# Routing turns on TensorE: float32 products with the identity in place of transposes

## The reference

```python
h = layernorm(x)
theta = relu(mean(gcn(h, edges)))            # one vector of 64
coefs = ...sigmoid(theta @ W2 + b2)...       # [256, 4]: two scales, two shifts per channel
x = x + max(h * scale0 + shift0, h * scale1 + shift1)      # per channel
h = layernorm(x)
top, idx = top_k(h @ gate_w + gate_b, 2)     # 16 experts
y = h + sum_k softmax(top)_k * (relu(h @ w1[idx_k] + b1) @ w2[idx_k] + b2)
x = x + layernorm(y) * gamma + beta
```

## Time and profile before

| what | us |
|---|---|
| three timed runs | 886.05, 889.9, 895.62 (median 889.9) |
| span of the profiled execution, first to last instruction | 882.4 |
| TensorE busy, matmul records / weight loads | 741.0 / 643.2 |
| VectorE / ScalarE / GpSimd busy | 676.2 / 475.4 / 282.7 |
| mean granted clock of TensorE over the span, as a share of full speed (no time) | 0.913 |

### The profile page before, as it was taken

One profiled execution on the slowest core, in us unless ns is written; L12 is line 12 of the kernel. 1 busy time (PEld: TensorE's weight loads), 2 busy tenths in 40 slices (PEclk: granted clock), 3 DMA queues, 4 the chain that ended last, 5 costly groups with the idle time before them and its releaser, 6 DMA issues.

```text
span 882.4 us, 21305 instructions
## 1 busy us (share of the span) xinstructions
PE 741.0 (84%) x6322; PEld 643.2 (73%) x6322; DVE 676.2 (77%) x1837; ACT 475.4 (54%) x1199; POOL 282.7 (32%) x313
## 2 busy tenths in 40 slices
PE   3555788888885776897899999999999999998893
PEld 3555355555555765876889999999998999997682
DVE  6999699999963688776757777777776777775597
ACT  5995677777635675653334444444444444443253
POOL 8400000000000457777734544544422222223010
PEclk9999699999997676568999999999999999999796
DMA  9850444445616944459999999899999999893999
GB/s 270 223 162 1 130 148 152 165 142 175 172 64 237 227 133 145 128 152 292 254 278 280 267 264 263 266 264 261 269 254 335 323 260 273 262 262 116 353 319 200
DMA packets 156240, 192.82 MB, mean 219 GB/s; under 512 B 78235, under 2 KB 125262, under 8 KB 153036
## 3 DMA queue, kind: packets, MB, share of 16 engines
q1 hardware_dynamic: 127048, 109.40, 44.7%
q10 hardware_dynamic: 15448, 51.04, 17.4%
q0 software_dynamic: 13632, 31.03, 11.2%
HBM read 151.05 MB, written 40.34 MB: 217 GB/s over the span
## 4 chain that ended last, share of the span: by engine, by line
PE 60%; DVE 23%; issue 8%; DMA 3%; ACT 3%; SPq 2%; DVEq 0%; ACTq 0%; POOL 0%; POOLq 0%
PE PS L1296 21%; PE PS L1308 19%; DVE W L1357 8%; PE PS L1334 4%; DVE W L1388 3%; DVE W L1423 3%; PE PS L1090 3%; PE PS L1186 2%; PE PS L1201 2%; DMA R<-xs 2%; PE PS L1214 2%; PE PS L1110 2%; SPq L719 2%; PE PS L1054 1%; DVE st L1464 1%
## 5 line engine op out<-in xcount | busy, mean ns | idle before, releaser
L1296 PEld LDWEIGHTS PS<-R,W 128*128 128x128 f32 x1808 | 223.1, 195 | 17.2 <-DVE R L1640 11.9
L1296 PE MATMUL PS<-R,W 128*128 128x128 f32 x1808 | 225.1, 278 | 9.7 <-DVE R L1640 9.7
L992 ACT ACTIVATE R<-PS,b1T 128x128 f32<-128x128 f32 x350 | 102.9, 367 | 233.9 <-PE PS L1296 233.8
L1308 PE MATMUL PS<-W,R 128*128 x904 | 213.9, 380 | 0.0
L610 POOL DMA_INDIRECT ys<-W,R x113 | 109.7, 971 | 230.9 <-DVE W L1692 228.5
L1308 PEld LDWEIGHTS PS<-W,R 128*128 128x128 f32 x904 | 163.6, 191 | 17.4
L1357 DVE TENSOR_TENSOR W<-R,W 128x3136 bf16<-128x3136 bf16 (+1 forms) x104 | 157.2, 1571 | 0.7 <-PE PS L1070 0.7
L890 ACT ACTIVATE W<-PS 128x1024 f16<-128x1024 f32 x104 | 106.2, 1023 | 38.0 <-PE PS L1090 32.0
L603 POOL DMA_INDIRECT xs<-W,slot_i x98 | 101.8, 1039 | 75.0 <-DVE slot_i L1522 46.3
L1090 PE MATMUL PS<-W,table 114*128 114x512 f16 x208 | 66.3, 403 | 26.3 <-DVE W L1388 25.9
L595 POOL MEMSET R<- 128x261 f32 x1 | 0.3, 317 | 226.4 <-PEq L1132 226.4
(11 more groups left out here) (264 smaller groups left out, 1028.9 us busy)
## 6 DMA issues: line engine op xcount, KB each, us to landing
W<-in_L_ffn_w ACTq DMA_DIRECT2D x96, 512.0 KB, 5.0
W<-key_rows SPq DMA_DIRECT2D x26, 784.0 KB
W<-in_L_ffn_w SPq DMA_DIRECT2D x33, 512.0 KB, 8.5
R<-xs SPq DMA_DIRECT2D x113, 130.5 KB
W<-ys SPq DMA_DIRECT2D x4, 2048.0 KB, 13.0
R<-xs SPq DMA_DIRECT2D x224, 32.0 KB
XH<-in_x SPq DMA_DIRECT2D x6, 896.0 KB, 11.7
W<-xs SPq DMA_DIRECT2D x116, 32.0 KB
```

Of the source, the lines that this page charges most:

```text
L992: last = act.activation(HT3[:, u, j, :], up_out(u, j), ACT.Relu, bias=b1T[:, ds(e, 1), j])
L1296: last = nc.tensor.matmul(up_out(u, j), W1S[b][:, k, j * P:(j + 1) * P], XT3[:, u, k, :], start=(k == 0), stop=(k == 1))
L1308: last = nc.tensor.matmul(PS[:, 6 * u, 0:C], HT3[:, u, j, :], wt2(e * W2COLS, j), start=(j == 0), stop=(j == 3))
```

## The change: what it does

The three calls of `nc.tensor.transpose` in `turn1`, `back` and `turn2` become `nc.tensor.matmul` with the same three operands (the block as the stationary side, the 128x128 float32 identity as the moving side). A transpose is that product with a flag set; now the flag is left out, and each turn is an ordinary float32 product. Operands, PSUM places, waits, signals and the order on each engine stay as they were. Other transposes of the program (in the graph stage and in `turn_tables`) stay as they were too.

```diff
-                            last = nc.tensor.transpose(TA[q % 2][:, j, k, :], XH[:, DG[g][0] + j0 + j, k * P:(k + 1) * P], ident[:, :])
+                            last = nc.tensor.matmul(TA[q % 2][:, j, k, :], XH[:, DG[g][0] + j0 + j, k * P:(k + 1) * P], ident[:, :],
+                                                    start=True, stop=True)
...
-                            last = nc.tensor.transpose(TB[:, j, k * P:(k + 1) * P], bra[q % 2][:, k, j, :], ident[:, :])
+                            last = nc.tensor.matmul(TB[:, j, k * P:(k + 1) * P], bra[q % 2][:, k, j, :], ident[:, :],
+                                                    start=True, stop=True)
...
-                            last = nc.tensor.transpose(PS[:, 6, j * C + k * P:j * C + (k + 1) * P],
-                                                       xn[:, g % XNBUFS, 2 * b + j, k * P:(k + 1) * P], ident[:, :])
+                            last = nc.tensor.matmul(PS[:, 6, j * C + k * P:j * C + (k + 1) * P],
+                                                    xn[:, g % XNBUFS, 2 * b + j, k * P:(k + 1) * P], ident[:, :],
+                                                    start=True, stop=True)
```

## The result

| | before, on the same chip | after |
|---|---|---|
| median of four timed runs, us | 887.97 (884.33 to 895.62) | 906.02 (901.56 to 914.89) |
| span of the profiled execution, us | 882.4 | 905.3 |
| its own timed value, us | 884.33 | 907.03 |
| mean granted clock over the span | 0.913 | 0.940 |

The account below looks back on a forecast made before the run. The routing stage was taken as bound by TensorE at a mostly half clock. Turns +5.6, gates -5.5 and cold starts +2.6 gave +2.7 us on 889.9: 892.5 us, range 882 to 909.

Parts of the forecast that it names:

- half clock behind 360 us: Sign of being wrong: the profile after still shows half clock there, where near 1.00 was expected from 340 to 390 us.
- the last `back`: End of the routing stage's turns: expected within 4 us of where it was, at 383.93 us before.
- The bound: Routing stage, 262 to 455 us: bound by TensorE more than any other engine, at a clock mostly half; expert steps follow.
- Turns and gates: Routing chain: 230 turns as full-clock products plus hand-over tails, +5.6 us; 109 gate records cheaper at full clock, -5.5 us.
- Cold starts: Products beginning at half clock after long waits at three places, 0.9 us each: +2.6 us, bounds 0 and 5.2.
- The rival that the clock falls at every `back`: Routing stage: each of 13 `back`s on the chain starts and stays cold, 18.6 us more, 908.5 us; chance 0.13.
- The rival that the clock's pattern stays: From 262 to 390 us the mean clock stays 0.645, products cost 40.8 us more, gates gain nothing: 931 us; chance 0.10.
- GpSimd's sends: Back to back from 330.09 to 434.85 us: ending some 4 us later, ahead of the fourteenth step's need, costed at nothing.

Follow-up runs that it names:

- experiment 1: Products of zeros put in TensorE's waits of the routing stage, in the changed kernel: 896.76 us, ratio 1.007 to the kernel before.
- experiment 5: Changed kernel, waits filled, 18 zero products ahead of the last group: 893.76 us, ratio 1.0036; transposes likewise, plus 14 before the second expert step: 878.75 us, 0.9847.
- experiment 2: The same products of zeros in the same waits, in the kernel before with its transposes: 886.54 us, ratio 0.9894.
- `turn2` alone: Only `turn2`'s 98 turns made products, in the kernel before: 901.75 us, ratio 1.0099.

## Why the prediction was right in its range and wrong in its sum, step by step

The time lies in the range (882 to 909), but 13.5 us above the forecast and outside the forecast's own bounds (885 to 900). The range holds it only because it was widened for a rival that had 0.13, with other places and prices than the runs showed; that is luck in good part. Slower by over 1%, which came, had 0.23. Of the signs of being wrong, half clock behind 360 us came (0.50 from 362.54 us to 373.76), and the last `back` begins 12.6 us later, not within 4.

**The bound** was read rightly: the stage is limited by TensorE, and what the last `back` lost, the expert steps lost with it.

**Turns and gates** (+5.6 and -5.5 us). The prices held: 16 records in 1.95 us to their end, gates at 0.96 us for eight. With the clock held by fillers the change costs 0.36% of the median, 3.2 us, where these two terms sum to +0.1; its stage is 2.0 us longer than before. So experiments 1 and 5 bear the two terms out together, to some 2 or 3 us, with the fillers' own cost included; neither was measured alone.

**Cold starts** (+2.6 us, bounds 0 and 5.2) is the step that failed, by size. It measured 11.1 us in the stage (after against experiment 1) and about 3 at the last group (experiment 1 against 5), 14 in all. Put in place of 2.6, the forecast's sum of 2.7 becomes 14.1 us; by the ratio the change costs 16 us, by the medians 18, and the two stretches ahead of the second expert step differ by 16.1. Three things in it were wrong:

- The places. I took three, `back` at 275 and behind `fill_soon` and the first `prefix`, and all three fell. Three more did, at 329, 346 and 387, behind waits of 2.28, 1.87 and 3.25 us. I had argued from the expert steps, which kept 1.00 over waits of 1 to 2 us up to 445 us. The next wait behind that window, of 2.20 us, already speaks against it (before, from the timeline):

```profile
445.93 3.55 PE L1296 MATMUL PS<-R,W 128*128 128x128 f32 x16 [2.20 <-DVE R L1640]
```
- The length. I took half of one `back`'s 1.73 us. The fall at 362 lasted from `back` through the gates, `turn1` and the next `back`, 11 us.
- The work already there for this. Of `spin` I had only named that it exists. At full clock the same eight products end 1.7 us sooner, the wait behind them opens, and the clock falls where before it had just come up.

**What would have been seen from the rows ahead.** The rival that the clock falls at every `back` (908.5 us) came nearest to the time, with 0.13; it had too many places (of the 15 `back`s, 6 fell behind a wait), and made each too short. Its 13 waits of 1 to 5 us were misread, too: the timeline of before has 11, of 0.45 to 4.78 us, and 7 of them reach 1 us. The rival that the clock's pattern stays (931 us) is refuted by the windows of after. The Trainium skill (Perfetto Trace Analysis, section Transposes) asks for transposes rather than products for every logical transpose. At equal fillers the runs agree: 1.018 in time for the products (experiments 1 and 2). What I had weighed was a turn at the clock of before against a product at full clock; the runs show that the turn gains from fillers as well, though its clock is held less well, and then it is the cheaper one.

**GpSimd's sends** at nothing: the last one is issued at 449.24 us, against 434.85, and the fourteenth `up`, the first whose rows wait for the sends, takes 1.95 us at 471.64 with no wait ahead in TensorE's timeline. That held.

**What stays open**: some 2 to 4 us of the cost, which lie in the price of the turns, in the expert steps or in the scatter of the medians; why waits of 1.87 and 2.28 us lose the clock and one of 2.63 us doesn't; and why the clock of `turn2` alone falls below that of before.

## What to carry to other kernels

When an edit is to pay through the clock, first price what the old form gains when the clock is raised in another way: here, with the same fillers, the transposes were ahead by some 1.8%, although their clock still fell at times. Waits of 1.9 to 6 us between short stretches of mixed work on TensorE cost the clock in six places here, and the price of a fall is all the work until the clock climbs, not one instruction; filling such waits with products of zeros gave 1.5% on the kernel as it was. Whatever already keeps the clock up (here `spin`) is sized for the clock that it finds, and must be sized anew when that changes.

## What the runs showed of the hardware that was not expected

- Turns lose the clock in work that products hold it through. In experiment 2 it falls at 298 us while TensorE works without a gap. In experiment 1, with the same fillers ahead, the same gates stand between products and keep their full-clock length, as does the `back` behind them:

```profile
302.32 0.96 PE L1223 MATMUL PS<-gw_sb,W 128*128 128x16 f32 x8
303.17 0.71 PE L1208 MATMUL PS<-ident,W 128*128 128x128 f32 x4
303.72 0.96 PE L1223 MATMUL PS<-gw_sb,W 128*128 128x16 f32 x8
304.53 1.58 PE L1192 MATMUL PS<-ident,W 128*128 128x128 f32 x12
```

  From 304 to 390 us the mean clock is 1.00 with products and 0.82 with turns, so the narrow gates alone don't lose it. The Trainium skill (TensorE: Matmul & The Clock Gate, Part 4: PE-mode transpose) says that transposes don't count as busy for the clock in the same way, and that full speed doesn't engage for them. This pair agrees with the first; the second is too strong for this case, as the next point shows.
- Turns themselves run at full clock where it is held: eight in 1.08 us at 330.78 before.
- Products don't always get the clock back soon: from 362.54 to 373.76 us after, products with one row of gates between them ran at half clock for 11 us without a gap, while behind the `back` at 275.41 us, of the same 16 records, the next turns already had full-clock length. What makes the difference was not tested.
- With the 58 products of `turn1` on the chain the clock is higher in all three windows, and the time is as before (ratio 0.9984), while the 86 of `back`, or the 86 of `turn2`, cost 1% each.
